# First-half root from its own rows, and the low parts of the shared weights moved between engines in the opening of a two-layer gated attention and expert kernel

## The reference

```
x = x + tanh(g_xattn[0]) * xattn(layernorm(x), ctx, ctx, mask)
#   scores = hidden @ ctx.T, masked;  softmax over the 77;  weights @ ctx
x = x + tanh(g_ffn[0]) * ffn(layernorm(x), ...)
#   z = (silu(xt @ ws1.T + bs1) * (xt @ ws3.T + bs3)) @ ws2.T + bs2   (shared expert, 512 wide)
#   y = weighted sum over the two best of eight experts
```

## Time and profile before

| | us |
|---|---|
| median of three runs | 593.8 (593.31 to 593.92) |
| the profiled execution, whole | 596.97 |
| its span, first to last instruction | 595.1 |
| PE busy | 564.3 (95%) |
| DVE busy | 452.2 (76%) |
| ACT busy | 377.0 (63%) |
| GpSimd busy | 257.5 (43%) |

### The profile page before, as it was taken

The page is one execution under the profiler, slowest core; times in us unless marked ns, Lnnn a source line. Parts: engine busy times, 40 slices in busy tenths (PEclk is TensorE's granted clock), DMA queues, the critical chain, the costliest instruction groups (busy, mean ns, idle before and its releaser), DMA issues.

```text
span 595.1 us, 12930 instructions
## 1 busy us (share of the span) xinstructions
PE 564.3 (95%) x3952; PEld 466.0 (78%) x3952; DVE 452.2 (76%) x1246; ACT 377.0 (63%) x729; POOL 257.5 (43%) x291
## 2 busy tenths in 40 slices
PE   8989999999999999999999999979889999999997
PEld 8778898888879999999999988867545555655654
DVE  4878788787765877788888864668988898868755
ACT  4666787666644777777777763345664784775633
POOL 4436555565460234555443445666635551310100
PEclk9979999999999999999999999999999999999999
DMA  8225444562248778879998827462112420200000
GB/s 236 86 94 192 165 166 143 165 234 107 81 169 282 268 250 264 273 251 270 271 292 261 274 84 293 140 219 81 46 44 72 140 91 37 72 1 36 36 37 35
DMA packets 47973, 93.15 MB, mean 157 GB/s; under 512 B 6990, under 2 KB 17306, under 8 KB 47778
## 3 DMA queue, kind: packets, MB, share of 16 engines
q1 hardware_dynamic: 39740, 74.34, 37.5%
q0 software_dynamic: 7440, 17.97, 10.0%
q10 hardware_dynamic: 726, 0.02, 0.1%
HBM read 61.32 MB, written 32.17 MB: 157 GB/s over the span
## 4 chain that ended last, share of the span: by engine, by line
PE 52%; DVE 21%; ACT 8%; issue 7%; DMA 4%; POOL 4%; SPq 3%; ACTq 0%; DVEq 0%; POOLq 0%
PE bank L1343 11%; PE bank L1345 10%; PE bank L1344 10%; PE bank L1838 6%; PE bank L1281 4%; PE bank L1859 3%; DVE st L2414 3%; PE bank L1860 2%; POOL yr L736 2%; DVE xa L2405 2%; DVE g3l L2491 2%; DMA wraw<-in_wexp 2%; DVE sl L2486 2%; DMA rows_by_expert<-n,pos 2%; DVE x L2047 1%
## 5 line engine op out<-in xcount | busy, mean ns | idle before, releaser
L640 POOL DMA_INDIRECT rows_by_expert<-n,pos x64 | 64.3, 1005 | 52.0 <-DVE pos L2142 35.5
L688 POOL TENSOR_TENSOR yg<-yg,b 128x512 f32<-128x512 f32 x31 | 46.2, 1492 | 90.0 <-ACT yg L828 90.0
L736 POOL DMA_INDIRECT yr<-expert_out,out_row x64 | 65.3, 1020 | 31.1 <-issue 18.4
L1838 PE MATMUL bank<-m4Th,wint 128*128 128x512 f16 x192 | 69.1, 380 | 4.6 <-DVE sl L2486 2.6
L1343 PE MATMUL bank<-xTh,wph 128*128 128x256 f32 x248 | 72.3, 291 | 1.1 <-DVE wpl L2307 0.8
L1345 PE MATMUL bank<-xTh,wpl 128*128 128x256 f32 x248 | 70.1, 283 | 0.0
L1344 PE MATMUL bank<-xTl,wph 128*128 128x256 f32 x248 | 70.1, 283 | 0.0
L1838 PE MATMUL bank<-m4Tl,wint 128*128 128x512 f16 x192 | 68.8, 379 | 0.0
L2307 DVE TENSOR_TENSOR wpl<-wraw,wph 128x1024 fp32r<-128x1024 f32 x40 | 49.0, 1225 | 12.7 <-ACT wph L828 12.6
L828 ACT ACTIVATE wph<-wraw 128x1024 fp32r<-128x1024 f32 x40 | 42.3, 1058 | 16.0 <-PE bank L1345 9.8
L2486 DVE SCALAR_TENSOR_TENSOR sl<-bank,sl 128x512 f32<-128x512 f32 x48 | 33.1, 689 | 21.8 <-ACT sl L1142 21.5
(11 more groups left out here) (350 smaller groups left out, 1750.6 us busy)
## 6 DMA issues: line engine op xcount, KB each, us to landing
wraw<-in_wexp SPq DMA_DIRECT2D x40, 512.0 KB, 4.5
xg<-rows_by_expert SPq DMA_DIRECT2D x31, 256.0 KB, 4.1
expert_out<-yg SPq DMA_DIRECT2D x31, 256.0 KB, 3.1
x_shared<-x SPq DMA_DIRECT2D x8, 512.0 KB, 2.8
xa<-x_shared SPq DMA_DIRECT2D x4, 1024.0 KB, 6.7
out<-ost SPq DMA_DIRECT2D x8, 512.0 KB, 2.8
xin<-in_x SPq DMA_DIRECT2D x7, 512.0 KB, 3.9
stage<-in_wexp SPq DMA_DIRECT2D x8, 256.0 KB, 3.9
```

What stands on the lines that cost most here:

```text
L640: pool.indirect_dma_start(out=xs, out_offset=bass.IndirectOffsetOnAxis(ap=pos[p][:, k, j:j + 1], axis=0), in_=n2[p][:, j, :], in_offset=No ...
L688: pool.tensor_tensor(yg[u % 3], yg[u % 3], b2[:, bass.ds(e, 1), :].broadcast_to([P, 2, D]), ALU.add)\
L736: pool.indirect_dma_start(out=yr[:, c, k, j, :], out_offset=None, in_=ys, in_offset=bass.IndirectOffsetOnAxis(ap=out_row[:, b * GB + c, k, ...
L1838: last = mm(bank[:, 2 * (m % 2) + w, :], wt[:, k, m * P:(m + 1) * P], part[c][:, k, :], start=(q == 0 and k == 0), stop=(q == 1 and k == K ...
```

## The change

It alters the opening in four ways. The root of the first half is formed from the statistics of the first two tiles alone, under its own semaphores (`half_stats`, `half_var`, `half_rstd`), and the second half's after it; each is a GpSimd `tensor_scalar` and a `pow` of 128 x 2 in place of one pair of 128 x 4. GpSimd no longer forms the low parts of tiles 0 and 1; DVE forms them after `row_max_half(1)`. DVE forms that of tile 2 no longer there but after `ln2_stats_half(0)`, and ACT its high part not before but after the first half's `pt_copy_half`. GpSimd forms the low parts of tiles 4 and 5 only after `rstd_half(1)` and after `row_max(1)`.

```diff
--- before.py
+++ after.py
@@ -596,11 +596,20 @@
                 chained(pool.iota(ints[0:parts, 0:n], pattern, base=0, channel_multiplier=mult))
                 chained(pool.tensor_copy(dst, ints[0:parts, 0:n]))
 
+            def opening_rstd(h, stats, var, rstd):
+
+                n = slice(2 * h, 2 * h + 2)
+                pool.wait_ge(sem(stats), 1)
+                pool.tensor_scalar(ve[0][:, n], mv[0][:, n, 1], EPS, None, ALU.add).then_inc(sem(var), 1)
+                pool.wait_ge(sem(var), 1)
+                pool.tensor_tensor(rstd1[0][:, n], ve[0][:, n], halfpow[:, n], ALU.pow).then_inc(sem(rstd), 1)
+
             def rstd_first(g):
 
                 pool.wait_ge(sem("stats0"), g + 1)
-                if g:
-                    pool.wait_ge(sem("rstd0"), g)
+                pool.wait_ge(sem("rstd0"), g)
+                if g == 1:
+                    pool.wait_ge(sem("half_rstd"), 1)
                 pool.tensor_scalar(ve[0], mv[0][:, :, 1], EPS, None, ALU.add).then_inc(sem("var0"), 1)
                 if g >= 2:
                     pool.wait_ge(sem("probs_done"), GT * (g - 1))
@@ -652,13 +661,13 @@
                 scatter(f, 1 - p, (1,), first)
                 scatter(f, 1 - p, (1,), second)
 
-            rstd_first(0)
-            shared_low(0, 1)
-            shared_low(1, 1)
+            opening_rstd(0, "half_stats", "half_var", "half_rstd")
+            opening_rstd(1, "stats0", "var0", "rstd0")
             rstd_half(0)
             rstd_first(1)
+            rstd_half(1)
+            pool.wait_ge(sem("negmax_done"), 2 * halves(1))
             shared_low(4, 2)
-            rstd_half(1)
             shared_low(5, 2)
             pool.memset(zeros, 0.0).then_inc(sem("filled"), 1)
             pool.memset(ones8, 1.0).then_inc(sem("filled"), 1)
@@ -990,12 +999,12 @@
             t1_copy_half(1)
             for c in range(2):
                 stage_high(c, wsh[:, c, :], 1)
-            stage_high(2, wsh[:, 2, :], 1)
             act.wait_ge(sem("small_in"), 16 * 6)
             act.activation(gains, gains_raw, ACT.Tanh).then_inc(sem("gains_done"), 1)
             softmax_half(0)
             softmax_half(1)
             pt_copy_half(0)
+            stage_high(2, wsh[:, 2, :], 1)
             t1_copy(1, (0, 3))
             pt_copy_half(1)
             for c in range(3):
@@ -1994,7 +2003,7 @@
                 s = bank[:, 6 - 4 * h, 0:2 * P].rearrange("p (j n) -> p j n", j=2)[:, :, 0:KV]
                 dve.tensor_reduce(negmax[:, n], s, AX.X, ALU.max, negate=True).then_inc(sem("negmax_done"), 1)
                 dve.wait_ge(sem("negmax_done"), 2 * h + 1)
-                dve.wait_ge(sem("rstd0"), 1)
+                dve.wait_ge(sem("rstd0" if h else "half_rstd"), 1)
                 tt(negmax[:, n], negmax[:, n], rstd1[0][:, n], ALU.mult).then_inc(sem("negmax_done"), 1)
 
             def prob_scale(g):
@@ -2206,6 +2215,10 @@
                     dve.wait_ge(sem("x_in0"), 16)
                 for j in range(2 * h, 2 * h + 2):
                     dve.bn_stats(st[0][:, j, :], xin[0][:, j, :]).then_inc(sem("bn0"), 1)
+                for j in range(2 * h, 2 * h + 2):
+                    dve.wait_ge(sem("bn0"), j + 1)
+                    ins = dve.bn_aggr(mv[0][:, j, :], st[0][:, j, :])
+                ins.then_inc(sem("stats0" if h else "half_stats"), 1)
                 if h == 0:
                     dve.wait_ge(sem("ctx_mean"), 1)
                     tt(ctxC[:, :, 0, :], ctxT[:, 0, :, :], bank[:, 6, 0:KV].unsqueeze(1).broadcast_to([P, KD, KV]), ALU.subtract)\
@@ -2213,11 +2226,11 @@
                     dve.wait_ge(sem("mask_in"), 16)
                     ts(barred[0:1].rearrange("p b s -> p (b s)"), maski, 0.0, NEG, ALU.is_equal, ALU.mult)\
                         .then_inc(sem("mask_ready"), 1)
-            ln_sums(0, 0)
             dve.wait_ge(sem("pool_const"), 18)
             row_max_half(0)
             row_max_half(1)
-            low_part(2, wsh[:, 2, :], wsl[:, 2, :], 1)
+            low_part(0, wsh[:, 0, :], wsl[:, 0, :], 1)
+            low_part(1, wsh[:, 1, :], wsl[:, 1, :], 1)
             dve.wait_ge(sem("gains_done"), 1)
             prob_scale_half(0)
             chained(cp(gw[:, :, 0:NE], gwf))
@@ -2236,6 +2249,7 @@
 
             residual_half(0)
             ln2_stats_half(0)
+            low_part(2, wsh[:, 2, :], wsl[:, 2, :], 1)
             ln1_stats(1, 1, 0)
             prob_scale_half(1)
             residual_half(1)
```

## The result

| | before | after |
|---|---|---|
| median of 20 runs each, us | 593.51 (592.17 to 596.64) | 597.44 (592.61 to 600.25) |
| ratio, with 95% interval | | 1.0052 (1.0036 to 1.0068) |
| profiled execution, us | 596.97 | 597.78 |
| its span, us | 595.1 | 595.9 |

The changed kernel is slower by 3.9 us by the medians, by 3.1 by the ratio. The two profiled executions differ by only 0.8 us. That gap between the profiles and the medians is explained further down.

The account below looks back on a forecast made before the run. The prediction took PE, busy 95% of the span, and the opening's chain of waits as the bound. Load wait 2.4 plus clock 1.7 gave 4.1 us, added to the median: 597.9 us, range 595.2 to 600.0.

Parts of the forecast that it names:

- What goes at first, 0: First root and first softmax: softmax starts some 0.4 us earlier but waits for PE, added work is hidden; effect 0.
- The load of tile 5: Tile 2's later low part delays this load; ACT waits, and second norm and PE's transposes come 3.2 and 3.0 us later.
- The recovered stretch of DVE, 0.6 back: At group 1's softmax, ACT's 0.61 us wait for DVE's row maximum goes, cutting the 3.0 us delay to 2.4.
- The clock, 1.7: PE's 2.7 us idle before the second norm's transposes likely drops its clock; cost 0 to 3.4 us, middle taken.
- The bias split, 0: GpSimd's two low parts now run beside DVE's bias split; all but 0.2 us is covered, so cost taken as 0.
- 0 to 1.08: Bound in us on what GpSimd's two low parts beside the bias split can cost on DVE.
- the way to the end: Behind 30 us steps are chained and PE is nearly always busy, so the whole 4.1 us delay passes to the end.
- 601.1: Forecast profiled execution of the changed kernel in us: 596.97 before plus 4.1.
- the later dip: Before's clock fall after PE's 1.67 us idle ahead of L1310, around 39 to 46 us: 6.8 us at 1.2 GHz.
- the later dip goes: Rival: no fall at the later idle time nor the new wait; up to 3.4 us back, 592.8 us; chance 0.12.
- my 2.4: Delay in us of group 1's softmax, second norm and PE's transposes from the load wait: 3.0 less 0.6.

Follow-up runs that it names:

- e7: The kernel before with 22 short, unused identity products on PE ahead of the second norm's transposes; 606.67 us beside 606.97 before, ratio 1.0008.
- e3: The changed kernel with 22 short, unused identity products on PE ahead of the second norm's transposes; 594.83 us, ratio to before 1.0010.
- e1: The changed kernel with ACT's high part of tile 5 moved behind the second norm's first half and its copy; 593.81 us, ratio to before 0.9986.
- e5: e1 with GpSimd's low parts of tiles 4 and 5 moved behind the bias split; 603.51 us beside 606.97 before, ratio 0.9943.
- e9: The kernel before with the divided root alone, all low and high parts left in place; 593.75 us, ratio to before 0.9973.
- e2: The kernel before with only DVE's low part of tile 2 moved behind the second norm's statistics; 597.82 us, ratio to before 1.0063.
- e6: The changed kernel with both parts of tile 2 back at their old places; 605.51 us beside 606.97 before, ratio 0.9978.
- e4: The kernel before with only GpSimd's low parts of tiles 4 and 5 moved behind both roots and group 1's row maximum; 594.93 us, ratio 1.0019.
- e8: The changed kernel run again unaltered, on the second chip; 608.97 us, ratio to before 1.0023.
- e10: The changed kernel run a third time unaltered, on the third chip; 596.35 us, ratio to before 1.0021.
- e11: e3 run again, on the third chip beside e10; 594.78 us, ratio to before 1.0000.
- e12: e5 run again, on the third chip; 592.94 us, ratio to before 0.9973.

## Why the prediction was right, point by point

Predicted were 597.9 us (595.2 to 600.0) and "slower" with 0.84; measured 597.4.

- **What goes at first, 0**: right in this profile. The first exponentials start at 10.12, half a microsecond earlier, and the products on the identity start at 11.42 on the chain as before, the residual at 16.07. DVE's added low parts end at 13.17 (11.88 + 1.29). It is not right for every run. This profile has PE at half speed in the opening, and in some runs PE is at full speed there (last section). Then PE's queue is short and waits for ACT's first softmax, which waits for GpSimd's root and the stretched multiplication. So in e7, where both stand as in the kernel before:

```profile
9.08 1.16 DVE L1999 TENSOR_TENSOR negmax<-negmax,rstd 128x2 f32<-128x2 f32 x1 [0.77 <-POOL rstd L609]
```

```profile
11.33 0.32 PE L1281 MATMUL bank<-identr,probsr 128*77 128x128 f32 x2 [1.45 <-ACT probs L871]
```

  and in e3, with the changed order, where PE waits for a load of x instead:

```profile
9.71 0.37 PE L1290 MATMUL bank<-identr,probsr 128*77 128x128 f32 x2
11.28 0.88 PE L1290 MATMUL bank<-identr,xin1r 128*128 128x128 f32 x8 [0.70 <-DMA xin<-in_x]
```

  The residual starts at 13.24, 13.19 and 13.57 us in e1, e3 and e5, and at 13.96 and 14.12 in e7 and e9, which keep GpSimd's first low parts (in e2, too, but its clock fell at 13.3 us). By these five profiles the change gains 0.4 to 0.9 us ahead of x in such runs, which the forecast put at 0 and the table, counted from x, cannot show.
- **The load of tile 5**: right, link by link. Low part at 18.01 (forecast 18.30, the whole opening being 0.3 earlier), landing after 3.27 us (forecast 3.0, bounds 2.8 to 3.9), high part 0.63, norm at 22.55 (22.65), PE's transposes at 23.68 (23.75). Behind x, t2_half(0) came 3.25 us later; forecast 3.0. e1, e2 and e6 show that this link and no other makes the wait.
- **The recovered stretch of DVE, 0.6 back**: measured 0.81, as the distance of the two transposes before (11.66 - 4.36 = 7.30) less the one of e3 (6.49). The moved low parts are not its source. e7 leaves them where they were, its transposes of the first half come 2.54 us late, those of the second 1.72 (6.48 between them), and its multiplication takes 0.16 us, since GpSimd has finished before DVE comes to it. A delay of the second norm brings these 0.8 us back by itself.
- **The clock, 1.7**: measured 1.61. The fall itself was shorter than I had drawn it, 3.4 us in place of up to 6.8, but all of it lay under work on the path, at half speed. Half of 3.4 is 1.7: the middle of my range met the size by another product than mine, and that was luck.
- So t2_half(1), behind x: 3.25 - 0.81 + 1.61 = 4.05 us later; forecast 4.1.
- **The bias split, 0**: right for this kernel, where DVE has 1.46 us to spare. The cover is the new wait. In e1, e4 and e6, without it, the stretched split is on the path, about 1.1 us by e1 against e5. "0 to 1.08" was also too narrow a bound for the instructions: they lost 0.69 + 0.97 = 1.66 us.

**The step that was weak is the last, the way to the end.** I wrote 601.1 for a profiled execution and it was 597.78. Before's profiled execution holds the later dip, after's does not, and both have the idle time of 1.66 us ahead of it. Between the low rows and group 1's transposes lie 27.91 - 12.87 = 15.04 us with the dip and 29.41 - 16.91 = 12.50 without: 2.5 us come back. The clock is the reason: in the eight profiles without a fall there (after, e1, e3, e4, e6, e7, e8, e10) the stretch takes 12.47 to 12.50 us, in the six with one 13.82 to 15.04. That is the rival "the later dip goes", in the profiled execution, together with my forecast and not in its place. I had called it unlikely because the idle time would recur; it recurred, and the clock stayed up. Of the 4.05 us, 1.5 are left at group 1. Between kernels without a fall in that stretch the 4.05 would pass on whole, as I had let them. Further on the comparison is blurred again by after's second fall, at 72.4 us.

Why then do the medians differ by 3.9? Before's profiled execution stands 3.5 us above its median and after's 0.3 above its own. The likely reading is that many of before's runs have no later dip, so that "before" in the medians has less to lose than its profile; kernels that are the same as before at that place show it in some profiles and not in others (last section). Only a profiled execution has a trace, but the mean granted clock of each run bears this out. Of before's 35 runs beside e1 to e4, 15 are at 0.994 or below, as the profile with its fall of 6.8 us is, with a median of 595.7 us; 18 are at 0.996 or above, which leaves no room for such a fall, with a median of 593.1. So at least half of them are without it, and the two kinds differ by 2.7 us. For before's 20 runs of the result no clock is on record, so for them it stays argued. Adding 4.1 to the median came out right, but it rested on the dip being in both, which it was not.

**What stays open is the size.** The loss was 0.52% in the result, whose chip is not on record, and 0.23% and 0.21% on the second and third chip of the experiments (intervals 0.9990 to 1.0056 and 0.9998 to 1.0043). e2 alone gave 0.63% on the first. The traces of e8 and e10 have the delay in full all the same (15.72 and 16.06 against 11.66), so it is the runs that lose less by it. One reading is the clock again: on those two chips the changed kernel's mean granted clock is that of the kernel before (0.9890 against 0.9892, 0.9936 against 0.9931), so the new fall does not come on top of before's. In the result it is 0.9933, and before's 35 runs on the first chip have 0.9951. That is argued from means. e3 and e11, which keep the wait and lose only the fall, are level with before, so that the wait's share in the time is small or is made up by the 0.8 us that come back ahead of t2_half(1) and by what the change gains ahead of x; my 2.4 for it would be 0.40%, outside e3's interval by a little (upper end 1.0037) and outside e11's (1.0021). e7 agrees that part of such a delay is made up behind. The clock's 1.6 us would be 0.27%; the two pairs differ by 0.42% (the result and e3) and by 0.21% (e10 and e11), each give or take about 0.3%. Against e12 the wait without the fall cost 1.8 us, the fall 1.6 more. The mechanism is shown, and both its parts in the traces; that they add up to some 4 us in the medians holds for the result, and for e2, which has the wait alone.

## What to carry to other kernels

A staging buffer ties the start of its next load to its last reader, and the load's landing to whatever stands behind its next reader in another engine's queue. Before such a reader is moved, follow the buffer: when is the load issued then, who waits for it, and what unrelated work is queued behind that wait. Where one instruction of VectorE is freed from GpSimd, look at which one GpSimd's work lands beside next; and when a wait leaves TensorE idle, price the work right behind it at half clock.

## What the runs showed of the hardware

**Full clock comes at different times in the opening.** The four score products of the opening take 0.64 us in some profiles and 1.11 in others, with the granted clock given as 1.00 in both (four products of 77 columns each time). PE's timeline of e1, and of the changed kernel:

```profile
8.10 0.64 PE L1564 MATMUL bank<-ctxC,n1T 128*128 128x77 f32 x4
```

```profile
10.24 1.11 PE L1563 MATMUL bank<-ctxC,n1T 128*128 128x77 f32 x4
```

The long form is PE at 1.2 GHz: in the kernel before, four products of the same shape take 1.11 us at 39.19, where the granted clock is 0.50, and in e12, which starts with the short form, they take 1.12 us at 8.60, where its trace gives the clock as 0.50 (from 8.3 to 15.1 us). The short form came in e1, e2, e3, e5, e7 and e9, the long one in before, after, e4, e6, e8, e10 and e11. The residual starts at 13.2 to 15 us with the first and at 16 with the second and in e12. That is up to 3 us, of which at most 0.9 belong to an edit, and perhaps a good part of the 8 us over which 35 runs of one kernel spread (590.64 to 598.57). A granted clock of 1.00 in the first microseconds is no proof of full speed; the length of a known product is.

**The same idle time sometimes costs the clock and sometimes not.** After the 1.64 to 1.67 us ahead of group 2's scores the granted clock fell, at once or within some 3 us, in the profiles of before, e2, e5, e9, e11 and e12. It stayed up in those of after, e1, e3, e4, e6, e8 and e10 (in e7 it fell only 12 us later). After, e1 and e4 have a fall of 3.4 us at 72.4, 66.4 and 68.4 us, with PE busy 1.00 in each of the three microseconds before, so an idle time right ahead is not needed either. After the 2.92, 2.93 and 3.26 us of the changed kernel's three profiles it fell each time, and in these three it did not fall again at the later place; of the eleven other profiles six fell there. Whether the one fall keeps the other away, three profiles cannot say. The page "TensorE: Matmul & The Clock Gate" of the Trainium skill (section "HAM oscillation — how this bites in real kernels") describes a matrix engine that waits for a load and starts its next work at the low clock, and the changed kernel's three traces agree with that picture. Its rule speaks of longer idle times than any of these, so the measurements go further than the page: 2.92 to 3.26 us were enough three times of three, 1.64 to 1.67 sometimes. What decides there these runs do not show.

**A cast stands behind GpSimd too.** The cast of 3 x 256 from 32 to 16 bits, with one input, went from 0.27 to 0.96 us beside GpSimd's low parts. The two-input subtraction next to it went from 0.41 to 1.38.

**GpSimd stands behind VectorE as well.** In the changed kernel the root of the second norm starts while DVE forms the low part of tile 2 (18.01 to 18.69 us) and takes 1.13 us in place of 0.70. This is GpSimd's timeline:

```profile
18.11 1.13 POOL L634 TENSOR_TENSOR rstd<-ve,halfpow 128x2 f32<-128x2 f32 x1 [9.30 <-DVE negm L2041]
```

It is hidden there behind the load. In e1, e5 and e12, where nothing hides it, the norm starts 3.47 to 3.48 us behind x in place of 3.05. The low part of tile 2 behind the root is the next thing that I would try.

**A chip can be slower by 13 us as a whole.** The same kernel before took 593.81, 606.97 and 595.40 us on the three chips. Two things are seen in the traces of the second chip. The kernel before spends more time at the low clock there: its mean granted clock over 35 runs is 0.9892, against 0.9951 and 0.9931. And between 120 and 185 us all four profiles of that chip (e5 to e8) have waits of ACT of 8.0 to 10.8 us in all, and of DVE besides, that the trace puts down to another core or an unknown queue; none of the other ten profiles has one. The products themselves are not slower: those with 512 columns between 100 and 200 us take 369 ns in e5 as in e1, and 401 in e8, whose clock is at 0.50 for 13.7 us of that stretch (in e5 for none). What the waits are was not tried. It is a reason to compare only kernels that ran on the same chip.
